# Attention weights of a graph layer: one exponential of the shifted score, or the larger of two exponentials with a bias per partition

## The chip, the core and the metric

The kernel runs on one core of a Trainium2 chip. The metric is device time in microseconds; 2156.93 us is the median of three runs of the kernel before (2154.71 to 2158.30).

## What is computed

A block of a graph network on 1250 nodes and 41250 edges: a layer norm, then two graph attention layers beside a linear-attention mixer, then a layer of 32 experts. The change is in the first attention layer alone, in what follows its projection h = x W (four heads of 512 columns). Of the reference this is:

```
e = jax.nn.leaky_relu(al_s[src] + al_d[dst], NEG_SLOPE)      # slope 0.2
m = jax.ops.segment_max(e, dst, num_segments=N)
ex = jnp.exp(e - m[dst])
denom = jax.ops.segment_sum(ex, dst, num_segments=N)
alpha = ex / (denom[dst] + 1e-16)
msg = h[src] * alpha[:, :, None]
out = jax.ops.segment_sum(msg, dst, num_segments=N)          # then + b1, then elu
```

The kernel does this densely. A matrix of edge counts c[s, d] is made earlier; the weight of source s for destination d is c[s, d] * exp(leaky(al_s[s] + al_d[d]) - m[d]), and the sum over sources is a matrix product. A column of ones beside h gives the denominator.

## The kernel before

The phases of the program follow each other; within one, each engine has its own instruction queue, and semaphores connect them. The phase of the change is gat1_phase. It makes 40 tiles: 4 heads of 10 tiles t, each with P = 125 destinations. A global number g = 10 hd + t counts them. For a tile:

- SyncE (SP) loads the counts cnt of the tile, 125 sources by 10 groups by 125 destinations (L1194 by way of L101 and L102), and, a head ahead, two rows broadcast to all partitions: al_d and m for all 1250 nodes (load_rows, L1180 and L1182). At the start it loads the whole bias brow (L1177); in the first head it also loads the weights of the second layer (L1358).
- VectorE, scores: u = al_s + al_d row (L1231), the leaky maximum max(0.2 u, u) (L1233), e = u - m row (L1235). Each is one pass over 125x1250. al_s differs by partition and group, the rows by destination.
- ScalarE: e = exp(e) in place, one instruction of 125x1250 (L1290).
- VectorE, weights: wt = e * cnt (L1243), a fourth pass of 125x1250.
- TensorE, aggregate: Z = sum over the ten groups of wt times h, in two halves of 256 and 257 columns (L1327), 20 products of float32 (40 records in the trace).
- VectorE, normalise: 1/denominator (L1250, L1251), o = Z * that + bias (L1252, L1254), mn = min(o, 0) (L1258). ScalarE: exp(mn) (L1303). VectorE, elu: o = max(exp(mn) - 1, o) (L1263).
- TensorE, turn: four transposes of o (L1337). ScalarE: copy of them out of PSUM to oT (L1307), then it issues the store to h1T_dram (L1309).

The order in each queue is written out by hand. In step t, VectorE does scores(t+2), normalise(t), weights(t+2), elu(t); ScalarE the exponential of tile t+2 (exp_scores), exp(mn) of tile t, the copy of tile t; TensorE aggregate(t+1), turn(t). The e, wt, cnt, o, mn, Z and oT buffers are double. The function heads runs this for head 0, then for heads 1 and 2 in a hardware loop (Fori) with one pass, then for head 3. Its waits count: exp_scores(t) waits for e_ready, weights(t) for exp_done, aggregate(t) for w_ready, and ScalarE's copy of tile t for turned, which the transposes of tile t raise.

Of the kernel before, what the change touches and what calls it, by code (L numbers as in the profile page):

```python
# [15 lines left out]
NT = 10  # L16
# [1123 lines left out]
def gat1_phase(nc, cx, b1, h, al, alT_dram, mT_dram, c_dram, h1T_dram, ident, W2, wa2, w2, w2_loaded, ext_ready):  # L1140


    (e_ready, exp_done, w_ready, agg, mn_ready, exp_mn, elu_ready, turned, t_evac, dve_step, b_loaded) = (
        cx.sem("gat1_" + s) for s in
        ("e_ready", "exp_done", "w_ready", "agg", "mn_ready", "exp_mn", "elu_ready", "turned", "t_evac", "dve_step",
# [6 lines left out]
    with ExitStack() as st:  # L1152
        brow = sb(nc, st, "gat1_brow", [128, F1])
        rows = [sb(nc, st, f"gat1_rows{b}", [128, 2, N]) for b in range(2)]
        u = sb(nc, st, "gat1_u", [P, NT, P])
# [11 lines left out]
        def heads(eng, body):  # L1167

            body(0, 0, True, False)
            with eng.Fori(0, H1 // 2 - 1) as i:  # L1170
                body(i * 2 + 1, 1, False, False)
                body(i * 2 + 2, 0, False, False)
            body(H1 - 1, 1, False, True)

        @block.sync
        def _(sp):
            sp.dma_start(brow[:], b1.partition_broadcast(128)).then_inc(b_loaded, 16)  # L1177

# [19 lines left out]
            heads(sp, body)  # L1198
# [7 lines left out]
        def _(dve):  # L1206
            def steps(before):

                made = [0]

                def step(ins):
                    made[0] += 1
                    ins.then_inc(dve_step, 1)
                    dve.wait_ge(dve_step, before + made[0])
                return step

            STEPS = 5
# [3 lines left out]
            dve.wait_ge(b_loaded, 16)


            def scores(hd, t, hb):
                b, g = t % 2, hd * NT + t
                step = steps(2 * g if isinstance(g, int) and g < 2 else g * STEPS - 6)
                if t == 0:
                    dve.wait_ge(rows_loaded[hb], (hd - hb) * 16 + 32)
                if not (isinstance(g, int) and g == 0):
                    dve.wait_ge(e_ready, g)  # L1230
# [51 lines left out]
            heads(dve, body)  # L1282

        @block.scalar
        def _(act):
            act.sem_inc(t_evac, 2)

            def exp_scores(hd, t):
                act.wait_ge(e_ready, hd * NT + (t + 1))
                act.activation(e[t % 2][:], e[t % 2][:], ACT.Exp).then_inc(exp_done, 1)  # L1290
# [21 lines left out]
            heads(act, body)  # L1312
# [4 lines left out]
        def _(pe):  # L1317
# [3 lines left out]
            def aggregate(hd, t):  # L1321
# [28 lines left out]
            heads(pe, body)  # L1350
# [1257 lines left out]
```

## Time and profile before

| what | value |
|---|---|
| median of three runs | 2156.93 us |
| the profiled execution, its own time | 2157.98 us |
| its span in the trace | 2156.3 us |
| TensorE busy over the span | 2021.0 us (94%) |
| VectorE | 1202.9 us (56%) |
| ScalarE | 448.0 us (21%) |
| the phase of the change, bias load to last copy | 861.9 to 1247.7 us |

The trace is of one execution, taken by the hardware profiler; all its times are counted from the start of the span. The span lies 1.7 us below the execution's own time. A row in order of time gives the start, the length, the engine, the line, the operation and its tiles, and in brackets the idle time of the engine before it with what ended it. A row that merges several instructions ends in a count. Shares of busy time are means over phases with different limits; for the phase of the change, a table by stretches gives the busy time of each engine there. A busy TensorE is one whose records follow without a gap, with its granted clock beside it.

### The profile page before, as it was taken

What the parts mean: (1) busy time and instruction counts of PE and PEld (TensorE: products, weight loads), DVE (VectorE), ACT (ScalarE), POOL (GpSimd) and SP (SyncE); (2) the same over time, 40 slices, a digit from 0 to 9 for tenths busy, and PEclk for the clock granted to TensorE, in tenths of its full rate; (3) what the DMA queues carried; (4) which work ended last, traced back from release to release, by engine and by line L of the source; (5) the groups of instructions that cost most, each with busy time, mean ns of one, the idle gap of its engine ahead of it and who ended that gap; (6) DMA issues with size and microseconds to landing.
All of it is one profiled execution on the core that took longest, in us unless ns stands there. A gap on an engine that the chain in (4) does not pass through costs nothing. (4 is left out here: it accounts for less than half of the span.)

```text
span 2156.3 us, 33575 instructions
## 1 busy us (share of the span) xinstructions
PE 2021.0 (94%) x10041; PEld 1479.3 (69%) x10042; DVE 1202.9 (56%) x2661; ACT 448.0 (21%) x822; POOL 183.1 (8%) x179
## 2 busy tenths in 40 slices
PE   4999899999999999799999979988996999999998
PEld 3666566666656888688888845545654777777776
DVE  5766436764375662788888742146765333333343
ACT  2212212122102321122222200003331222222222
POOL 0000000000000000000000000001001233233232
PEclk9999899999999999899999989998996999999999
DMA  7000130002436430743333244333405888898754
GB/s 254 16 16 19 64 123 19 16 16 85 150 111 194 146 117 1 246 152 99 122 97 95 70 159 166 133 112 105 146 29 201 251 244 248 239 293 274 203 128 86
DMA packets 81182, 282.66 MB, mean 131 GB/s; under 512 B 11690, under 2 KB 32226, under 8 KB 71491
## 3 DMA queue, kind: packets, MB, share of 16 engines
q1 hardware_dynamic: 59282, 211.66, 29.6%
q0 software_dynamic: 14848, 56.18, 10.7%
q10 hardware_dynamic: 6960, 13.62, 1.8%
q8 instruction: 55, 0.90, 0.2%
q14 instruction: 37, 0.30, 0.0%
HBM read 217.43 MB, written 63.99 MB: 131 GB/s over the span
## 5 line engine op out<-in xcount | busy, mean ns | idle before, releaser
L1327 PE MATMUL gat_Z<-h,gat_wt 125*125 125x256 f32 (+1 forms) x1600 | 354.9, 380 | 17.8 <-DVE gat_wt L1243 17.8
L1327 PEld LDWEIGHTS gat_Z<-h,gat_wt 125*125 125x125 f32 x1600 | 297.5, 188 | 63.7 <-DVE gat_wt L1243 18.2
L732 PE MATMUL mix_G<-mix_w,xnT 128*125 128x384 f32 x720 | 243.7, 489 | 0.0
L732 PEld LDWEIGHTS mix_G<-mix_w,xnT 128*125 128x125 f32 x720 | 133.6, 190 | 85.4 <-issue 3.1
L2091 PE MATMUL gat_Z<-h,gat_wt 125*125 125x384 f32 (+1 forms) x400 | 135.4, 496 | 13.0 <-DVE gat_wt L1830 13.0
L2331 DVE TENSOR_SCALAR ex_idS<-ex_ids 128x1 int32 x52 | 8.0, 154 | 215.1 <-DMA out_rows<-ex_y,ex_idS 215.1
L639 DVE SCALAR_TENSOR_TENSOR mix_count_A<-count_ikey,count_off,keyT 128x512 f32 x120 | 90.2, 751 | 56.4 <-issue 48.4
L2091 PEld LDWEIGHTS gat_Z<-h,gat_wt 125*125 125x125 f32 x400 | 75.0, 191 | 66.5 <-DVE gat_wt L1830 13.6
L2418 PE MATMUL ex_PH<-ex_xT,w_and_experts 128*128 128x128 f32 x936 | 113.0, 280 | 1.7 <-issue 0.7
L2418 PE MATMUL ex_PH<-ex_xT,ex_w 128*128 128x128 f32 x936 | 111.0, 277 | 1.1 <-issue 0.2
L645 DVE TENSOR_SCALAR mix_count_B<-count_islo,sloT 128x314 f16 x480 | 112.0, 298 | 0.0
L2418 PEld LDWEIGHTS ex_PH<-ex_xT,w_and_experts 128*128 128x128 f32 x936 | 108.4, 195 | 2.7 <-issue 2.6
L2428 PE MATMUL ex_PY<-ex_w,ex_hT 128*128 128x384 f32 x312 | 107.5, 494 | 1.3 <-ACT ex_hT L2365 1.3
L2428 PE MATMUL ex_PY<-w_and_experts,ex_hT 128*128 128x384 f32 x312 | 107.6, 495 | 1.0 <-ACT ex_hT L2365 0.7
L2418 PEld LDWEIGHTS ex_PH<-ex_xT,ex_w 128*128 128x128 f32 x936 | 106.5, 192 | 1.8 <-issue 1.8
L2301 DVE SCALAR_TENSOR_TENSOR ex_Q<-posm,offs,ex_iota 125x1280 bf16<-125x1280 f32 x54 | 83.8, 1552 | 38.8 <-issue 38.8
L2280 POOL DMA_INDIRECT out_rows<-ex_y,ex_idS x52 | 82.6, 1588 | 268.2 <-DVE ex_y L2333 223.3
L780 PE MATMUL mix_count_S<-mix_count_B,mix_count_A 128*128 x480 | 87.5, 300 | 5.1 <-DVE mix_count_B L645 2.8
L1557 PE MATMUL gat2p_X<-w_and_experts,gat2p_hT 128*125 128x386 f32 x240 | 81.2, 495 | 11.3 <-DMA gat2p_hT<-h1T_dram 11.3
L2373 ACT ACTIVATE ex_y<-ex_PY,ex_gate 128x384 f32<-128x384 f32 x52 | 30.2, 581 | 276.6 <-DMA out_rows<-ex_y,ex_idS 235.1
L2428 PEld LDWEIGHTS ex_PY<-ex_w,ex_hT 128*128 128x128 f32 x312 | 57.1, 190 | 39.6 <-ACT ex_hT L2365 2.2
L2428 PEld LDWEIGHTS ex_PY<-w_and_experts,ex_hT 128*128 128x128 f32 x312 | 57.1, 190 | 39.4 <-ACT ex_hT L2365 1.9
(346 smaller groups left out, 2974.2 us busy)
## 6 DMA issues: line engine op xcount, KB each, us to landing
w_and_experts<-in_L_ffn_W SPq DMA_DIRECT2D x32, 1152.0 KB, 8.1
ex_w<-in_L_ffn_W SPq DMA_DIRECT2D x32, 1152.0 KB, 7.9
gat_cnt<-c_dram SPq DMA_DIRECT2D x50, 546.9 KB
h1T_dram<-gat_oT ACTq DMA_DIRECT2D x40, 250.0 KB
gat2p_hT<-h1T_dram SPq DMA_DIRECT2D x10, 1000.0 KB, 6.5
mix_w<-in_L_mix_qkv_w SPq DMA_DIRECT2D x6, 1152.0 KB, 13.1
ct_dram<-mix_count_out SPq DMA_DIRECT2D x40, 157.0 KB, 2.0
mix_w_slice<-in_L_gnn_W SPq DMA_DIRECT2D x6, 1024.0 KB, 12.1
```

Of the source, the lines that this page charges most:

```text
L639: dve.scalar_tensor_tensor(CA[:, bass.ds(s * RB, RB), :], ikey[:].unsqueeze(1).to_broadcast([128, RB, 128]), off[:, win:win + 1], keyT[:, ...
L645: last = dve.tensor_scalar(CB[:, bass.ds(s * RB + b, 1), :], islo[:].unsqueeze(1), sloT[:, bass.ds(r * RB + b, 1)], None, ALU.is_equal)
L732: last = pe.matmul(G[c][:], xnT[:, k, t * P:(t + 1) * P], w[:, k, c, :], start=(k == 0), stop=(k == KD - 1))
L780: last = pe.matmul(S[:], CA[:, bass.ds(s * RB + b, 1), :].rearrange("p o k -> p (o k)"), CB[:, bass.ds(s * RB + b, 1), :].rearrange("p o k ...
L1327: last = pe.matmul(Z[b][j][:], wt[b][:, s, :], h[0:P, bass.ds(hd, 1), s, j * HC:(j + 1) * HC + j], start=(s == 0), stop=(s == NT - 1))
L1557: last = pe.matmul(bank[:, 0:W], stationary[:, k * P:(k + 1) * P], moving[:, k, :], start=fresh and k == 0, stop=k == KH - 1, skip_group_c ...
L2091: last = pe.matmul(Z[b][j][:], wt[b][:, s, :], h2[:, s, 386 * j:386 * j + CW[j]], start=(s == 0), stop=(s == NT - 1))
L2280: pool.indirect_dma_start(out, bass.IndirectOffsetOnAxis(ap=idS[:, 0:1], axis=0), y[:], None, compute_op=ALU.add).then_inc(added, 16)
L2301: dve.scalar_tensor_tensor(Q[:], posm[:, :, bass.ds(e, 1)].to_broadcast([P, NT, SLOT]), 1.0 if first else offs[:, bass.ds(at, 1)], iot[:]. ...
L2373: act.activation(y[:, 384:768], PY[1][:], ACT.Copy, scale=gate[:, slot]).then_inc(y_a, 1)
L2418: last = pe.matmul(PH[m][:], w1[b][:, k, m * 128:(m + 1) * 128], xT[:, k, :], start=(k == 0), stop=(k == KD - 1))
L2428: last = pe.matmul(PY[j][:], hT[:, k, :], w2[b][:, k, j * 384:(j + 1) * 384], start=(k == 0), stop=(k == KM - 1))
```

## The change

The weight is written another way. exp is increasing, so exp(max(u, 0.2 u) - m) is the larger of exp(u - m) and exp(0.2 u - m). With u = al_s + al_d these are exp(al_s + (al_d - m)) and exp(0.2 al_s + (0.2 al_d - m)): in each group of sources al_s is one number per partition, which an instruction of ScalarE can take as its bias.

- Once a head, shifted_rows makes the rows al_d - m and 0.2 al_d - m out of the loaded rows, in place, with two VectorE passes of 128x1250; for the next head this stands in step 5, ahead of normalise(5). Once a phase, al02 = 0.2 al_s is made (125x40).
- exp_scores makes e and f, ten instructions each of 125x125, one for each group, with al or al02 as bias.
- VectorE's scores are gone. weights first takes the larger of e and f, waits for it, and then multiplies by cnt.
- The bias is loaded a head at a time (128x512 in place of 128x2048), the next head's in step 5; VectorE waits for it in the first normalise of a head and no longer at the start. The rows of the head after next wait for the exponentials of a head (exp_done) in place of its scores (e_ready).
- The head loop is written out for all four heads, on all engines.

```diff
-        def heads(eng, body):
-
-            body(0, 0, True, False)
-            with eng.Fori(0, H1 // 2 - 1) as i:
-                body(i * 2 + 1, 1, False, False)
-                body(i * 2 + 2, 0, False, False)
-            body(H1 - 1, 1, False, True)
+        def heads(body):
+
+            for hd in range(H1):
+                body(hd, hd % 2, hd == 0, hd == H1 - 1)
...
-            sp.dma_start(brow[:], b1.partition_broadcast(128)).then_inc(b_loaded, 16)
+            def load_bias(hd):
+                sp.dma_start(brow[:, hd % 2, :], b1[hd * C1:(hd + 1) * C1].partition_broadcast(128)).then_inc(b_loaded, 16)
+
+            load_bias(0)
...
-                        sp.wait_ge(e_ready, hd * NT)
+                        sp.wait_ge(exp_done, hd * NT)
                     load_rows(hd + 1, 1 - b)
                 for t in range(NT):
+                    if t == NT // 2 and not last:
+                        if not first:
+                            sp.wait_ge(mn_ready, hd * NT + 2)
+                        load_bias(hd + 1)
...
-                step(dve.tensor_tensor(u[:], al[:, :, bass.ds(hd, 1)].to_broadcast([P, NT, P]),
-                                       rows[hb][0:P, 0:1, t * P:(t + 1) * P].to_broadcast([P, NT, P]), ALU.add))
-                step(dve.scalar_tensor_tensor(u[:], u[:], SLOPE, u[:], ALU.mult, ALU.max))
-                dve.wait_ge(w_ready, g + 1)
-                dve.tensor_tensor(e[b][:], u[:], rows[hb][0:P, 1:2, t * P:(t + 1) * P].to_broadcast([P, NT, P]),
-                                  ALU.subtract).then_inc(e_ready, 1)
+            step(dve.tensor_scalar(al02[:], al[:, :, 0:H1], SLOPE, None, ALU.mult))
+
+            def shifted_rows(hd, hb):
+                dve.wait_ge(rows_loaded[hb], (hd - hb) * 16 + 32)
+                step(dve.scalar_tensor_tensor(rows[hb][:, 1, :], rows[hb][:, 0, :], SLOPE, rows[hb][:, 1, :], ALU.mult,
+                                              ALU.subtract))
+                dve.scalar_tensor_tensor(rows[hb][:, 0, :], rows[hb][:, 0, :], 1.0 - SLOPE, rows[hb][:, 1, :], ALU.mult,
+                                         ALU.add).then_inc(r_ready, 1)
 
             def weights(hd, t):
                 b, g = t % 2, hd * NT + t
                 dve.wait_ge(exp_done, g + 1)
                 dve.wait_ge(c_loaded[b], hd * (2 * HT16) + 32 * (t // 2 + 1))
+                step(dve.tensor_tensor(e[b][:], e[b][:], f[b][:], ALU.max))
                 dve.wait_ge(agg, g + 1)
                 dve.tensor_tensor(wt[b][:], e[b][:], cnt[b][:], ALU.mult).then_inc(w_ready, 1)
...
                 for t in range(NT):
-                    if t + 2 < NT:
-                        scores(hd, t + 2, hb)
-                    elif not last:
-                        scores(hd + 1, t + 2 - NT, 1 - hb)
-                    normalise(hd, t, max(0, t + 3 - NT) if last else 0)
+                    if t == NT // 2 and not last:
+                        shifted_rows(hd + 1, 1 - hb)
+                    normalise(hd, t)
...
             def exp_scores(hd, t):
-                act.wait_ge(e_ready, hd * NT + (t + 1))
-                act.activation(e[t % 2][:], e[t % 2][:], ACT.Exp).then_inc(exp_done, 1)
+                g, b = hd * NT + t, t % 2
+                act.wait_ge(r_ready, hd + 1)
+                act.wait_ge(w_ready, g + 1)
+                for s in range(NT):
+                    act.activation(e[b][:, s, :], rows[hd % 2][0:P, 0, t * P:(t + 1) * P], ACT.Exp, bias=al[:, s, hd:hd + 1])
+                    last = act.activation(f[b][:, s, :], rows[hd % 2][0:P, 1, t * P:(t + 1) * P], ACT.Exp,
+                                          bias=al02[:, s, hd:hd + 1])
+                last.then_inc(exp_done, 1)
```

How the queues stand, first ScalarE in its steady steps. Before: the exponential of the tile two ahead, exp(mn), the copy of the turned tile, its store, and the next step's exponential.

```order
L1290 ACTIVATE gat_e<-gat_e 125x1250
L1303 ACTIVATE gat_mn<-gat_mn 125x512
L1307 ACTIVATE gat_oT<-gat_T 128x500
L1309 DMA h1T_dram<-gat_oT 128x500
L1290 ACTIVATE gat_e<-gat_e 125x1250
```

ScalarE after, from the last two of a tile's twenty exponentials to the first two of the next tile's (al02 shows as gat_al).

```order
L1279 ACTIVATE gat_e<-gat_rows,al 125x125
L1280 ACTIVATE gat_f<-gat_rows,gat_al 125x125
L1295 ACTIVATE gat_mn<-gat_mn 125x512
L1299 ACTIVATE gat_oT<-gat_T 128x500
L1301 DMA h1T_dram<-gat_oT 128x500
L1279 ACTIVATE gat_e<-gat_rows,al 125x125
L1280 ACTIVATE gat_f<-gat_rows,gat_al 125x125
```

Between one store and the next exp(mn), one instruction has become twenty; exp(mn), copy and store keep their places.

VectorE in a steady step, before: three passes of scores, five instructions of normalise, weights, elu.

```order
L1231 TENSOR_TENSOR gat_u<-al,gat_rows 125x1250
L1233 SCALAR_TENSOR_TENSOR gat_u<-gat_u 125x1250
L1235 TENSOR_TENSOR gat_e<-gat_u,gat_rows 125x1250
L1250 TENSOR_SCALAR gat_rden<-gat_Z 125x1
L1251 RECIPROCAL gat_rden<-gat_rden 125x1
L1252 SCALAR_TENSOR_TENSOR gat_o<-gat_Z,gat_rden,gat_brow 125x256
L1254 SCALAR_TENSOR_TENSOR gat_o<-gat_Z,gat_rden,gat_brow 125x256
L1258 TENSOR_SCALAR gat_mn<-gat_o 125x512
L1243 TENSOR_TENSOR gat_wt<-gat_e,gat_cnt 125x1250
L1263 SCALAR_TENSOR_TENSOR gat_o<-gat_mn,gat_o 125x512
```

The same step after.

```order
L1238 TENSOR_SCALAR gat_rden<-gat_Z 125x1
L1239 RECIPROCAL gat_rden<-gat_rden 125x1
L1240 SCALAR_TENSOR_TENSOR gat_o<-gat_Z,gat_rden,gat_brow 125x256
L1242 SCALAR_TENSOR_TENSOR gat_o<-gat_Z,gat_rden,gat_brow 125x256
L1246 TENSOR_SCALAR gat_mn<-gat_o 125x512
L1228 TENSOR_TENSOR gat_e<-gat_e,gat_f 125x1250
L1230 TENSOR_TENSOR gat_wt<-gat_e,gat_cnt 125x1250
L1251 SCALAR_TENSOR_TENSOR gat_o<-gat_mn,gat_o 125x512
```

The three passes ahead of normalise are gone, and a pass (the maximum of e and f) stands between normalise and the multiply, ahead of elu.

## Rows read from the trace of the kernel before

**Rows 1.** Stretches: us; busy PE, PEld, DVE, ACT, POOL; granted clock; DMA share, GB/s.
```profile
960.00:1040.00 80.00, 80.00 (x389) 69.19 (x388) 69.72 (x90) 21.16 (x27) 0.00 (x0) 1.00 0.34 103
```

**Rows 2.** One tile in time: start, us, engine, line, operation [idle before <-releaser].
```profile
1080.03 8.82 PE L1327 MATMUL gat_Z<-h,gat_wt 125*125 125x256 f32 x40
...
1080.22 0.59 ACT L1307 ACTIVATE gat_oT<-gat_T 128x500 f32<-128x500 f32 x1 [6.33 <-PE gat_T L1337]
...
1081.21 1.25 ACT L1290 ACTIVATE gat_e<-gat_e 125x1250 f32<-125x1250 f32 x1 [0.40 <-ACT gat_oT L1307]
1082.37 0.61 ACT L1303 ACTIVATE gat_mn<-gat_mn 125x512 f32<-125x512 f32 x1
1082.49 1.46 DVE L1243 TENSOR_TENSOR gat_wt<-gat_e,gat_cnt 125x1250 f32<-125x1250 f32 x1 [0.97 <-ACT gat_e L1290]
1083.87 0.69 DVE L1263 SCALAR_TENSOR_TENSOR gat_o<-gat_mn,gat_o 125x512 f32<-125x512 f32 x1
...
1088.68 0.59 PE L1337 MATMUL gat_T<-ident,gat_o 125*128 125x125 f32 x4
...
1089.31 0.59 ACT L1307 ACTIVATE gat_oT<-gat_T 128x500 f32<-128x500 f32 x1 [6.33 <-PE gat_T L1337]
```

**Rows 3.** The same view: copy of tile 0, and the last tiles.
```profile
898.53 0.59 ACT L1307 ACTIVATE gat_oT<-gat_T 128x500 f32<-128x500 f32 x1 [6.41 <-PE gat_T L1337]
...
1234.64 0.59 ACT L1307 ACTIVATE gat_oT<-gat_T 128x500 f32<-128x500 f32 x1 [6.33 <-PE gat_T L1337]
...
1245.72 0.69 DVE L1263 SCALAR_TENSOR_TENSOR gat_o<-gat_mn,gat_o 125x512 f32<-125x512 f32 x1 [0.70 <-ACT gat_mn L1303]
...
1246.47 0.65 PE L1337 MATMUL gat_T<-ident,gat_o 125*128 125x125 f32 x4 [2.78 <-DVE gat_o L1263]
1247.15 0.59 ACT L1307 ACTIVATE gat_oT<-gat_T 128x500 f32<-128x500 f32 x1 [1.46 <-PE gat_T L1337]
```

**Rows 4.** The same view: the start of the stage.
```profile
861.92 0.36 SPq L1177 DMA_DIRECT2D gat_brow<-in_L_gnn_b  x1
...
870.83 1.46 DVE L1231 TENSOR_TENSOR gat_u<-al,gat_rows 125x1250 f32<-125x1250 f32 x1 [9.83 <-DMA gat_rows<-mT_dram]
872.33 1.46 DVE L1233 SCALAR_TENSOR_TENSOR gat_u<-gat_u 125x1250 f32<-125x1250 f32 x1
...
878.37 19.69 PE L1327 MATMUL gat_Z<-h,gat_wt 125*125 125x256 f32 x80 [17.83 <-DVE gat_wt L1243]
...
889.73 0.15 DVE L1250 TENSOR_SCALAR gat_rden<-gat_Z 125x1 f32<-125x1 f32 x1
```

**Rows 5.** ScalarE by shape: line, shapes, count | busy us, mean ns | idle before.
```profile
L2365 ACT ACTIVATE ex_hT<-ex_PH,ex_b1T 128x128 f32<-128x128 f32 x156 | 54.0, 366 | 101.9 <-PE ex_PH L2418 91.8 <-issue 10.1
L1290 ACT ACTIVATE gat_e<-gat_e 125x1250 f32<-125x1250 f32 x40 | 49.9, 1246 | 44.2 <-DVE gat_e L1235 29.0 <-ACT gat_oT L1307 15.2
...
L1303 ACT ACTIVATE gat_mn<-gat_mn 125x512 f32<-125x512 f32 x40 | 24.6, 614 | 1.9 <-DVE gat_mn L1258 1.9
...
L308 ACT ACTIVATE xn<-xa,shift,rstd 125x768 f32<-125x768 f32 x10 | 10.0, 1021 | 7.3 <-DVE shift L240 7.3
...
L2055 ACT ACTIVATE rt_gate<-rt_gate 125x128 f32<-125x128 f32 x1 | 0.3, 292 | 0.0
```

**Rows 6.** In order of time, ScalarE alone: three neighbours merged into one row.
```profile
20.53 2.87 ACT L308 ACTIVATE xn<-xa,shift,rstd 125x768 f32<-125x768 f32 x3 [7.26 <-DVE shift L240]
```

**Rows 7.** Table by stretches around two idle gaps of TensorE, columns as rows 1.
```profile
556.00:557.70 1.70, 0.01 (x1) 0.01 (x1) 1.01 (x3) 0.00 (x0) 0.00 (x0) 1.00 0.00 0
557.70:559.00 1.30, 1.27 (x10) 1.30 (x11) 0.41 (x1) 0.41 (x1) 0.00 (x0) 0.78 0.19 26
559.00:562.50 3.50, 3.50 (x10) 2.29 (x9) 0.69 (x2) 0.56 (x2) 0.00 (x0) 0.59 1.03 227
...
1755.80:1757.10 1.30, 0.02 (x1) 0.00 (x0) 1.01 (x5) 0.82 (x3) 0.00 (x0) 1.00 1.01 428
1757.10:1760.00 2.90, 2.90 (x13) 2.05 (x14) 1.93 (x5) 0.95 (x3) 2.44 (x2) 1.00 1.05 367
```

More of the change, by code:

```diff
@@ L1140, in gat1_phase @@
 def gat1_phase(nc, cx, b1, h, al, alT_dram, mT_dram, c_dram, h1T_dram, ident, W2, wa2, w2, w2_loaded, ext_ready):
[L1143 removed]
+    (r_ready, exp_done, w_ready, agg, mn_ready, exp_mn, elu_ready, turned, t_evac, dve_step, b_loaded) = (
         cx.sem("gat1_" + s) for s in
[L1145 removed]
+        ("r_ready", "exp_done", "w_ready", "agg", "mn_ready", "exp_mn", "elu_ready", "turned", "t_evac", "dve_step",
          "b_loaded"))
@@ L1152, in gat1_phase @@
     with ExitStack() as st:
-        brow = sb(nc, st, "gat1_brow", [128, F1])
+        brow = sb(nc, st, "gat1_brow", [128, 2, C1])
         rows = [sb(nc, st, f"gat1_rows{b}", [128, 2, N]) for b in range(2)]
-        u = sb(nc, st, "gat1_u", [P, NT, P])
+        al02 = sb(nc, st, "gat1_al02", [P, NT, H1])
+        f = [sb(nc, st, f"gat1_f{b}", [P, NT, P]) for b in range(2)]
         e = [sb(nc, st, f"gat1_e{b}", [P, NT, P]) for b in range(2)]
@@ L1206, in _ @@
         def _(dve):
[L1207 to L1217, printed above, removed]
+            step = Chain(dve, dve_step)
             for freed in (w_ready, mn_ready):
                 dve.sem_inc(freed, 2)
[L1221 to L1230, printed above, removed]
-                step(dve.tensor_tensor(u[:], al[:, :, bass.ds(hd, 1)].to_broadcast([P, NT, P]),
-                                       rows[hb][0:P, 0:1, t * P:(t + 1) * P].to_broadcast([P, NT, P]), ALU.add))
-                step(dve.scalar_tensor_tensor(u[:], u[:], SLOPE, u[:], ALU.mult, ALU.max))
-                dve.wait_ge(w_ready, g + 1)
-                dve.tensor_tensor(e[b][:], u[:], rows[hb][0:P, 1:2, t * P:(t + 1) * P].to_broadcast([P, NT, P]),
-                                  ALU.subtract).then_inc(e_ready, 1)
+            step(dve.tensor_scalar(al02[:], al[:, :, 0:H1], SLOPE, None, ALU.mult))
[5 more added lines that the diff above has]
+                                         ALU.add).then_inc(r_ready, 1)
             def weights(hd, t):
@@ L1241, in weights, with normalise @@
                 dve.wait_ge(c_loaded[b], hd * (2 * HT16) + 32 * (t // 2 + 1))
+                step(dve.tensor_tensor(e[b][:], e[b][:], f[b][:], ALU.max))
                 dve.wait_ge(agg, g + 1)
                 dve.tensor_tensor(wt[b][:], e[b][:], cnt[b][:], ALU.mult).then_inc(w_ready, 1)
-            def normalise(hd, t, left):
+            def normalise(hd, t):
                 b, g = t % 2, hd * NT + t
-                step = steps(g * STEPS + (6, 4, 2)[left])
+                if t == 0:
+                    dve.wait_ge(b_loaded, 16 * (hd + 1))
                 dve.wait_ge(agg, g + 3)
@@ L1252, in normalise @@
                 dve.scalar_tensor_tensor(o[b][:, 0:HC], Z[b][0][:], rden[b][:],
-                                         brow[0:P, bass.ds(hd * C1, HC)], ALU.mult, ALU.add)
+                                         brow[0:P, hd % 2, 0:HC], ALU.mult, ALU.add)
                 step(dve.scalar_tensor_tensor(o[b][:, HC:C1], Z[b][1][:, 0:HC], rden[b][:],
-                                              brow[0:P, bass.ds(hd * C1 + HC, HC)], ALU.mult, ALU.add))
+                                              brow[0:P, hd % 2, HC:C1], ALU.mult, ALU.add))
                 if not (isinstance(g, int) and g == 0):
@@ L1263, in elu @@
                 dve.scalar_tensor_tensor(o[b][:], mn[b][:], -1.0, o[b][:], ALU.add, ALU.max).then_inc(elu_ready, 1)
+            shifted_rows(0, 0)
             for t in range(2):
-                scores(0, t, 0)
                 weights(0, t)
```

10 lines of the change are left out of this document (5 added, 5 removed).

## The prediction

> **What bounds the kernel now.** I read the views in this order: a table by stretches for the stage of the change, one steady tile of it in order of time, its first and last tiles, then the rows that price ScalarE instructions.
>
> The table [rows 1] shows 80 us from the middle of the first aggregation: TensorE is busy for all 80.00 us at a granted clock of 1.00 (2.4 GHz), VectorE for 69.72, ScalarE for 21.16. So VectorE is loaded to 87% but does not set the pace, and passes taken from it are not time taken from the kernel, unless something downstream of VectorE is late.
>
> One tile in order of time [rows 2] shows why nothing is late. The copy of the turned tile (L1307) starts at 1080.22 and the next one at 1089.31: a period of 9.09 us. From [rows 3], (1234.64 - 898.53) / 37 = 9.08 us over 37 tiles. Inside it TensorE runs one product of 8.82 us and four transposes; VectorE and ScalarE work beside it, and ScalarE waits 6.33 us for the transposes.
>
> The same rows hold a second loop, which now has slack. ScalarE's queue takes, for tile t: exponential of tile t+2, exponential of mn(t), copy of the turned tile t. The copy waits for turn(t), so **the exponential of tile t+3 stands behind the copy of tile t, that is behind turn(t)**. VectorE's queue takes normalise(t+1), weights(t+3), elu(t+1); so elu(t+1) stands behind the weights, which wait for that exponential. And turn(t+1) on TensorE waits for elu(t+1). This closes: turn(t), copy, exponential, weights, elu, turn(t+1). Before the change, counted from the start of the copy [rows 2]: exponential starts at 0.99, elu at 1083.87 - 1080.22 = 3.65 and ends at 4.34. The product of TensorE ends only at 1088.85. The next transposes start at 8.46, so about 4.1 us of slack lie in the loop, and that is all that the change can add to it free of charge.
>
> **The change part by part.**
>
> *VectorE loses two passes a tile and keeps two.* Before: add, leaky maximum, subtract, multiply, each about 1.46 us. After: a maximum and a multiply, both two-tensor passes of 125x1250, for which the multiply's 1.46 us [rows 2] is the price. About 2.9 us a tile go. The passes that go lay between elu and the next normalise, outside the loop above, beside a busy TensorE; their removal is worth 0 in steady state. The maximum that comes is inside the loop, with a wait for its end before the multiply: 1.50 us from start to start, as the two dependent passes at 870.83 and 872.33 show [rows 4].
>
> *ScalarE gains.* One exponential of 125x1250 becomes twenty of 125x125, each with a bias read per partition. No row has that form on SBUF data, so I bound it. Below: the exponential of 125x128 without a bias operand took 292 ns [rows 5], and neighbours overlap: the three instructions at 20.53 take 2.87 us while one takes 1.02 [rows 6, 5], so start to start is (2.87 - 1.02) / 2 = 0.925 us and the overlap about 0.095. That gives 0.20 us start to start and 0.29 for one. Above: the same 125x768 instructions carry two per-partition operands; from 1250 and 512 elements [rows 5] one element costs (1246 - 614) / 738 = 0.856 ns, so 643 elements fewer leave 0.925 - 0.550 = 0.375 us start to start, 0.47 for one. One operand lies in the middle: 768 elements without operands would be 614 + 256 x 0.856 = 833 ns, two operands made it 1021, so one is worth 94 ns, and 125 elements with one come to 292 - 3 + 94 = 383 ns, near the 366 ns that the one-operand 128x128 instruction on PSUM data took [rows 5]. I take 0.383 for one and 0.290 start to start. Twenty: 19 x 0.290 + 0.383 = **5.89 us** in place of 1.25; by the bounds 4.09 and 7.60.
>
> The Trainium skill ("ScalarE: Activation LUTs", section "What ACT_TABLE_LOAD costs") states 280 ns + 0.833 ns an element for an instruction with a bias pointer and an overlap of about 93 ns, by which the twenty would take 5.92 us and the period below would be 11.2 us as well. The skill also has a rule that speaks against the change: "VectorE: DVE Perf Modes", section on the TRN2 errata, says that an operation on SBUF data pays a fixed time per instruction, so that one large tile pays once and many small tiles pay each time, and advises tiles of 512 elements or more. Rows 5 agree: 1250 elements in one instruction cost 1246 ns, ten times 128 elements would cost 2920.
>
> *The loop after.* Copy to first exponential 0.99 (as now, with the store's issue between), twenty exponentials 5.89, release 0.03 (1081.21 + 1.25 to 1082.49 [rows 2]), maximum 1.50, multiply to elu 1.38 (1082.49 to 1083.87), elu 0.69 [rows 3], release 0.06 and transposes to the next copy 0.68 (1246.41 to 1246.47 to 1247.15 [rows 3], where the transposes waited for elu as they would here). Sum 0.99 + 5.89 + 0.03 + 1.50 + 1.38 + 0.69 + 0.06 + 0.68 = **11.22 us**. That exceeds the 9.08 of TensorE, so the loop becomes the bound: 2.14 us a tile. The product still starts right behind the transposes, since its weights were made a period earlier, and then TensorE idles some 1.8 us until elu. mn's exponential, now behind the twenty, ends at 0.99 + 5.89 + 0.6 = 7.5, ahead of elu at 9.8: hidden by the two passes. The loop runs from the copy of tile 0 to the copy of tile 37 (the exponentials of tiles 3 to 39): 37 x 2.14 = **79.2 us**. By the bounds 9.42 and 12.93 us a period: 12.6 and 142.5.
>
> *The start.* VectorE began at 870.83 when the rows landed, TensorE at 878.37 [rows 4]: 7.54 us. After: two passes that shift the rows 2 x 1.49, twenty exponentials 5.89, release 0.03, maximum and multiply 2.99 make 11.9 us: +4.4. The bias load ahead of the rows shrinks, by its shape, from 1024 to 256 KB; 1024 + 1250 KB took the 8.91 us from 861.92 to 870.83, so 768 KB less are worth up to 768 / 2274 x 8.9 = 3.0 us, nothing if the other loads fill the gap. I take **+2.5**, between 1.4 and 4.4. The second tile's weights come 8.8 us after the first's, hidden by the first product (878.37 to 889.73, 11.36 us after an idle 17.83 [rows 4]).
>
> *Costed at nothing.* The row shift for the next head (two passes, three times) sits before normalise(5): it moves that from the head of a period by 3 us, while the weights behind it wait until 6.9 anyway; if the twenty took 2 us, that cover would be gone and it would cost 1 us, three times. On SP, the row loads of a head now wait for the last exponential of the head before instead of its scores, and cnt loads are queued behind; the cnt of that tile has one period, 11.2 us, to land, and in the start's rows 2274 KB took 8.9 us against 1250 + 625 KB here. The bias loads stand mid-head, before one cnt load, with their condition long true. The head loop written out four times: tiles cross the loop's ends at the same 9.08 us now [rows 3], so no branch time is there to win.
>
> *The sum.* 79.2 + 2.5 = 81.7 us on the profiled execution's own 2157.98 (its span is 2156.3; the median of the runs shown, 2156.93, is 1 us less): 2239.7, and against the median 2238.6. I predict **2239**.
>
> **The rivals.**
>
> *Exponentials nearly as cheap as without an operand* (the lower bound): period 9.42, 12.6 us and about 0.7 at the start: 2171. For it: the operand's price rests on a two-operand row. Against: 366 ns on the only one-operand row of this size.
>
> *No loss at all.* The place is the same loop; the point from which it decides is twenty exponentials in 5.89 - 2.14 = 3.75 us, 0.18 us each: then TensorE's 9.08 stays the bound, the start is even (11.9 - 2.1 - 3.0 against 7.54), and the time is 2157. Slack left over buys nothing, since TensorE was full already [rows 1]. Against it: the lower bound is 0.20.
>
> *No overlap*, or an operand at twice the price (the upper bound): period 12.93, 142.5 + 4: 2304. Against: the overlap is seen with operands [rows 6].
>
> *TensorE's clock falls in the new gaps.* After an idle 1.70 us the granted clock was 0.78 and then 0.59 for 3.5 us, means of its levels 2.4 and 1.2 GHz; after an idle 1.30 us it stayed 1.00 [rows 7]. The new gap of 1.8 is like the first. But a product at 0.59 for 3.5 us and 0.78 for 1.3 loses 1.7 us, about the gap itself, so it still ends before elu; only transposes of 0.65 at 0.78 lie on the path: 0.2 x 37 = 7 us. With every product as slow as the first (11.36), a period is 11.36 + 0.26 = 11.6 and the time 2254. It widens the range upward and decides nothing.
>
> **How the numbers follow.** Forecast with its clock variants 0.83; cheap exponentials 0.07; no loss 0.03; no overlap 0.07. The range goes from 2215 (0.26 us start to start, one at 0.355, an even start: period 10.63, +57) to 2262 (0.31 us, period 11.60, 4.4 at the start and the clock's 7: +104); what it leaves out of the rivals is 0.17. A measurement of this kernel can tell about 0.2% from no change, 4.3 us: faster 0.01, same 0.02, slower 0.97.
>
> **What would show it.** In the changed kernel's profile, copies of the turned tile 11.2 us apart; twenty exponentials in 5.9 us starting 1.0 us after each copy; VectorE's maximum waiting for them; TensorE idle some 1.8 us a tile before its transposes, released by elu; VectorE busy only near half of the stage. If exponentials start every 0.20 us or less, or the idle time of TensorE is not put down to elu, the forecast is wrong.

## The result and the profile after

The changed kernel takes 2241.57 us (median of four runs, 2238.03 to 2244.00), the kernel before 2156.55 beside it; the ratio is 1.0393, with a 95% interval of 1.0375 to 1.0411. It is slower by 85 us; 2239 was forecast. The profiled execution took 2238.03 us, its span is 2236.3, so the trace has 80.0 us more than that of before to account for. One of the ten runs of the reordered kernel below took 2703 us at a granted clock of 0.735 in place of 0.97; its ratio and interval are of the other nine.

One steady tile of the changed kernel in order of time (start, length, engine, line, operation, idle before it with its releaser), against [rows 2]:

```profile
1091.06 8.82 PE L1319 MATMUL gat_Z<-h,gat_wt 125*125 125x256 f32 x40
...
1091.26 0.59 ACT L1299 ACTIVATE gat_oT<-gat_T 128x500 f32<-128x500 f32 x1 [3.81 <-PE gat_T L1329]
...
1092.31 0.40 ACT L1279 ACTIVATE gat_e<-gat_rows,al 125x125 f32<-125x125 f32 x1 [0.46 <-ACT gat_oT L1299]
...
1097.83 0.38 ACT L1280 ACTIVATE gat_f<-gat_rows,gat_al 125x125 f32<-125x125 f32 x1
1098.12 0.61 ACT L1295 ACTIVATE gat_mn<-gat_mn 125x512 f32<-125x512 f32 x1
1098.24 1.46 DVE L1228 TENSOR_TENSOR gat_e<-gat_e,gat_f 125x1250 f32<-125x1250 f32 x1 [6.08 <-ACT gat_f L1280]
1099.74 1.46 DVE L1230 TENSOR_TENSOR gat_wt<-gat_e,gat_cnt 125x1250 f32<-125x1250 f32 x1
1101.12 0.68 DVE L1251 SCALAR_TENSOR_TENSOR gat_o<-gat_mn,gat_o 125x512 f32<-125x512 f32 x1
...
1101.86 0.65 PE L1329 MATMUL gat_T<-ident,gat_o 125*128 125x125 f32 x4 [1.97 <-DVE gat_o L1251]
...
1102.54 0.59 ACT L1299 ACTIVATE gat_oT<-gat_T 128x500 f32<-128x500 f32 x1 [3.81 <-PE gat_T L1329]
```

The copy of the turned tile (now L1299) stands at 1091.26 and 1102.54: a period of 11.28 us in place of 9.09. The chain between is the one foretold. The first exponential starts 1.05 us after the copy, the twentieth ends at 1098.21, the maximum starts 0.03 later, then multiply, elu and transposes, each released by the one before. The product of TensorE, 8.82 us as before, has ended at 1099.88, and TensorE idles 1.97 us until elu lets the transposes go. Copy to first exponential 1.05, exponentials 5.90, release 0.03, maximum 1.50, multiply 1.38, elu and release 0.74, transposes to copy 0.68: 11.28.

The table by stretches of the same kernel (columns as in [rows 1]):

```profile
960.00:1040.00 80.00, 69.55 (x314) 57.72 (x313) 35.41 (x56) 50.13 (x159) 0.00 (x0) 0.96 0.32 97
```

TensorE is busy for 69.55 us of 80 where it was busy for all of them [rows 1], at a mean granted clock of 0.96; VectorE has fallen from 69.72 to 35.41, ScalarE has risen from 21.16 to 50.13. No engine is full, as it is when a chain of waits sets the pace. Who waited for whom in the phase (us in total, times, longest):

```profile
DVE gat_e L1228 <- ACT gat_f L1280: 225.6, 39, 6.5
...
PE gat_T L1329 <- DVE gat_o L1251: 56.4, 38, 2.8
```

VectorE's maximum waited 225.6 us for the exponentials, and TensorE's transposes 56.4 us for elu. Before, VectorE waited for its exponential too, but for 0.97 us a tile [rows 2], and in the steady tiles the transposes followed the product without a gap [rows 1].

The start, the copy of tile 0, that of tile 37 and the last one, against [rows 3, 4]:

```profile
858.88 0.36 SPq L1176 DMA_DIRECT2D gat_brow<-in_L_gnn_b  x1
...
867.44 1.46 DVE L1219 SCALAR_TENSOR_TENSOR gat_rows<-gat_rows 128x1250 f32<-128x1250 f32 x1 [8.14 <-DMA gat_rows<-mT_dram]
...
870.43 0.40 ACT L1279 ACTIVATE gat_e<-gat_rows,al 125x125 f32<-125x125 f32 x1 [15.12 <-DVE gat_rows L1221]
...
876.36 1.46 DVE L1228 TENSOR_TENSOR gat_e<-gat_e,gat_f 125x1250 f32<-125x1250 f32 x1 [5.97 <-ACT gat_f L1280]
...
879.37 19.02 PE L1319 MATMUL gat_Z<-h,gat_wt 125*125 125x256 f32 x80 [21.90 <-DVE gat_wt L1230]
...
898.85 0.59 ACT L1299 ACTIVATE gat_oT<-gat_T 128x500 f32<-128x500 f32 x1 [6.63 <-PE gat_T L1329]
...
1316.91 0.59 ACT L1299 ACTIVATE gat_oT<-gat_T 128x500 f32<-128x500 f32 x1 [3.81 <-PE gat_T L1329]
...
1329.41 0.59 ACT L1299 ACTIVATE gat_oT<-gat_T 128x500 f32<-128x500 f32 x1 [1.46 <-PE gat_T L1329]
```

From the copy of tile 0 to that of tile 37 there are 418.06 us, 11.30 a tile, where before there were 336.11: **+81.95**. From the first load of the phase to the copy of tile 0 there are 39.97 us in place of 36.61: **+3.36**. The rest is outside: the phase began 3.04 us earlier in this execution, and what follows the last copy took 2.2 us less. In the runs below the phase begins anywhere from 855.4 to 861.7 with the same code ahead of it, and what follows the last copy takes 907.6 to 912.9 us in those whose expert phase does the same work, so neither is put down to the change. 81.95 + 3.36 - 3.04 - 2.2 is the 80.0, to the rounding.

### The profile page after: what moved, and what is told of

Read it like the earlier page. It is cut to its first block and busy times, and to the rows that moved or that the text cites. A ratio compares the mean times of both kernels' runs of the same rounds, so it can differ in the third digit from the quotient of the medians.

```text
span 2236.3 us, 34292 instructions
## 1 busy us (share of the span) xinstructions
PE 2045.3 (91%) x10041; PEld 1489.2 (67%) x10042; DVE 1101.5 (49%) x2590; ACT 634.8 (28%) x1582; POOL 182.2 (8%) x179
## 5 line engine op out<-in xcount | busy, mean ns | idle before, releaser
L1319 PE MATMUL gat_Z<-h,gat_wt 125*125 125x256 f32 (+1 forms) x1600 | 374.0, 395 | 21.9 <-DVE gat_wt L1230 21.9
L1319 PEld LDWEIGHTS gat_Z<-h,gat_wt 125*125 125x125 f32 x1600 | 311.0, 196 | 73.6 <-DVE gat_wt L1230 22.3
L1228 DVE TENSOR_TENSOR gat_e<-gat_e,gat_f 125x1250 f32<-125x1250 f32 x40 | 58.4, 1461 | 225.6 <-ACT gat_f L1280 225.6
L1279 ACT ACTIVATE gat_e<-gat_rows,al 125x125 f32<-125x125 f32 x400 | 154.3, 386 | 32.5 <-ACT gat_oT L1299 17.3
L1280 ACT ACTIVATE gat_f<-gat_rows,gat_al 125x125 f32<-125x125 f32 x400 | 153.7, 384 | 0.0
L2083 PEld LDWEIGHTS gat_Z<-h,gat_wt 125*125 125x125 f32 x400 | 75.0, 191 | 66.6 <-DVE gat_wt L1822 13.7
L639 DVE SCALAR_TENSOR_TENSOR mix_count_A<-count_ikey,count_off,keyT 128x512 f32 x120 | 90.2, 751 | 56.4 <-issue 48.5
```

Of the source, the lines that this page charges most:

```text
L639: dve.scalar_tensor_tensor(CA[:, bass.ds(s * RB, RB), :], ikey[:].unsqueeze(1).to_broadcast([128, RB, 128]), off[:, win:win + 1], keyT[:, ...
L1279: act.activation(e[b][:, s, :], rows[hd % 2][0:P, 0, t * P:(t + 1) * P], ACT.Exp, bias=al[:, s, hd:hd + 1])
L1280: last = act.activation(f[b][:, s, :], rows[hd % 2][0:P, 1, t * P:(t + 1) * P], ACT.Exp, bias=al02[:, s, hd:hd + 1])
L1319: last = pe.matmul(Z[b][j][:], wt[b][:, s, :], h[0:P, hd, s, j * HC:(j + 1) * HC + j], start=(s == 0), stop=(s == NT - 1))
L2083: last = pe.matmul(Z[b][j][:], wt[b][:, s, :], h2[:, s, 386 * j:386 * j + CW[j]], start=(s == 0), stop=(s == NT - 1))
```

## The experiments

The theory: the changed kernel's pace is that of the loop copy, twenty exponentials, maximum, multiply, elu, transposes, copy. The rivals: the longer written-out program costs time; the work of ScalarE as such does; TensorE itself is slower, by its clock.

### The head loop alone

```diff
-            body(0, 0, True, False)
-            with eng.Fori(0, H1 // 2 - 1) as i:
...
+            for hd in range(H1):
+                body(hd, hd % 2, hd == 0, hd == H1 - 1)
```

> The kernel before with nothing changed but the head loop, written out for four heads. The theory (the loop copy, twenty exponentials, maximum, multiply, elu, transposes sets the pace of the changed kernel): the loop's form has no part in the loss, so the time is that of before, 2157 us, within 4, and the copies of the turned tile stand 9.08 us apart. The rival (some of the 85 us comes from the longer instruction stream): 2160 us or more, with idle time of TensorE put down to no engine.

Measured: 2155.44 us against 2157.45 for the kernel before beside it, ratio 0.9992 (0.9979 to 1.0006). The copies of tiles 0 and 37 in order of time:

```profile
896.22 0.59 ACT L1304 ACTIVATE gat_oT<-gat_T 128x500 f32<-128x500 f32 x1 [6.10 <-PE gat_T L1334]
...
1232.33 0.59 ACT L1304 ACTIVATE gat_oT<-gat_T 128x500 f32<-128x500 f32 x1 [6.33 <-PE gat_T L1334]
```

336.11 us for 37 tiles, to the hundredth that of before. The written-out loop costs nothing and saves nothing that these runs can tell.

### The same work in another order

```diff
                     normalise(hd, t)
+                    elu(hd, t)
                     if t + 2 < NT:
                         weights(hd, t + 2)
                     elif not last:
                         weights(hd + 1, t + 2 - NT)
-                    elu(hd, t)
...
             exp_scores(0, 1)
+            exp_scores(0, 2)
...
-                    if t + 2 < NT:
-                        exp_scores(hd, t + 2)
-                    elif not last:
-                        exp_scores(hd + 1, t + 2 - NT)
...
                     act.activation(mn[b][:], mn[b][:], ACT.Exp).then_inc(exp_mn, 1)
+                    if t + 3 < NT:
+                        exp_scores(hd, t + 3)
+                    elif not last:
+                        exp_scores(hd + 1, t + 3 - NT)
```

> The changed kernel with the same instructions in another order: on ScalarE the exponential of mn(t) first, then the twenty exponentials of tile t+3 (one tile further ahead) and then the copy of the turned tile t; on VectorE elu(t) ahead of weights(t+2). The theory: the twenty exponentials and the two passes leave the loop, TensorE is the bound again at 9.08 us a tile, and only the later start (about 4 us) stays: 2161 us, between 2156 and 2166. The rival (ScalarE's or VectorE's work as such, or its traffic, costs the time): ScalarE's 7.7 us of work a tile is the same, so the time stays near 2240.

Measured: 2158.24 us against 2157.45, ratio 1.0003 (0.9989 to 1.0017). The copies of the turned tile are 9.08 us apart (899.43 to 1235.54, 336.11 us for 37 tiles), and the loss is gone; the later start, 40.13 us from the first load to the copy of tile 0 against 36.61, is left and lies inside the interval. The table by stretches of this kernel:

```profile
960.00:1040.00 80.00, 80.00 (x389) 69.19 (x388) 47.94 (x74) 61.34 (x193) 0.00 (x0) 1.00 0.35 107
```

TensorE is full again at a clock of 1.00, with ScalarE at 61.34 us of 80, more than the changed kernel shows for the same stretch since it now makes a tile every 9.08 us. A tile in order of time:

```profile
1081.13 0.59 ACT L1300 ACTIVATE gat_oT<-gat_T 128x500 f32<-128x500 f32 x1 [1.26 <-PE gat_T L1330]
...
1082.46 0.63 ACT L1292 ACTIVATE gat_mn<-gat_mn 125x512 f32<-125x512 f32 x1 [0.75 <-DVE gat_mn L1246]
1083.00 0.39 ACT L1279 ACTIVATE gat_e<-gat_rows,al 125x125 f32<-125x125 f32 x1
1083.13 0.69 DVE L1251 SCALAR_TENSOR_TENSOR gat_o<-gat_mn,gat_o 125x512 f32<-125x512 f32 x1 [0.70 <-ACT gat_mn L1292]
...
1083.73 1.46 DVE L1228 TENSOR_TENSOR gat_e<-gat_e,gat_f 125x1250 f32<-125x1250 f32 x1
...
1085.22 1.46 DVE L1230 TENSOR_TENSOR gat_wt<-gat_e,gat_cnt 125x1250 f32<-125x1250 f32 x1
...
1088.50 0.39 ACT L1280 ACTIVATE gat_f<-gat_rows,gat_al 125x125 f32<-125x125 f32 x1
...
1089.58 0.59 PE L1330 MATMUL gat_T<-ident,gat_o 125*128 125x125 f32 x4
...
1090.21 0.59 ACT L1300 ACTIVATE gat_oT<-gat_T 128x500 f32<-128x500 f32 x1 [1.32 <-PE gat_T L1330]
```

exp(mn) comes first (1082.46), elu right behind it (1083.13), the maximum does not wait since the exponentials of its tile were made a step earlier, and the twenty that run from 1083.00 to 1088.89 are for the tile after. They end before the transposes at 1089.58 that release the next copy. The same twenty instructions, in the same number, cost 82 us in one order and nothing in the other. So neither ScalarE's work nor its traffic is the cause; the place in the queue is. The bias loaded a head at a time, the later wait of the row loads and the row shift are all in this kernel as well, so they cost no time a tile either. Three moves were made together here; the next experiment takes VectorE's apart from ScalarE's two, which were not tried one by one.

### One of the moves alone

```diff
                     normalise(hd, t)
+                    elu(hd, t)
                     if t + 2 < NT:
                         weights(hd, t + 2)
                     elif not last:
                         weights(hd + 1, t + 2 - NT)
-                    elu(hd, t)
```

> The changed kernel with one move alone: on VectorE elu(t) ahead of weights(t+2); ScalarE's order as it is. The theory: elu no longer waits for the two passes, but its exponential still stands behind the twenty, and the weights now come after elu. The pace is then set by a loop over two tiles: copy, exponentials, elu, maximum, multiply, product, transposes. 1.05 + 5.90 + 0.62 + 0.70 + 1.50 + 1.50 + 8.82 + 0.65 is 20.7 us for two tiles, 10.4 us for one: 1.3 above 9.08, so 48 us and 4 at the start, 2209 us, between 2198 and 2222. The rival (elu's place is what the loop hangs on alone): 2161.

Measured: 2206.73 us against 2157.45, ratio 1.0223 (1.0191 to 1.0255). Two tiles in order of time:

```profile
1066.97 0.59 ACT L1299 ACTIVATE gat_oT<-gat_T 128x500 f32<-128x500 f32 x1 [5.79 <-PE gat_T L1329]
...
1073.83 0.61 ACT L1295 ACTIVATE gat_mn<-gat_mn 125x512 f32<-125x512 f32 x1
...
1074.47 0.69 DVE L1251 SCALAR_TENSOR_TENSOR gat_o<-gat_mn,gat_o 125x512 f32<-125x512 f32 x1 [6.20 <-ACT gat_mn L1295]
...
1075.08 1.46 DVE L1228 TENSOR_TENSOR gat_e<-gat_e,gat_f 125x1250 f32<-125x1250 f32 x1
...
1076.06 0.59 ACT L1299 ACTIVATE gat_oT<-gat_T 128x500 f32<-128x500 f32 x1 [1.62 <-PE gat_T L1329]
1076.57 1.46 DVE L1230 TENSOR_TENSOR gat_wt<-gat_e,gat_cnt 125x1250 f32<-125x1250 f32 x1
...
1078.09 8.92 PE L1319 MATMUL gat_Z<-h,gat_wt 125*125 125x256 f32 x40 [2.07 <-DVE gat_wt L1230]
...
1087.47 0.59 ACT L1299 ACTIVATE gat_oT<-gat_T 128x500 f32<-128x500 f32 x1 [3.95 <-PE gat_T L1329]
```

From copy to copy two tiles on, 1066.97 to 1087.47, there are 20.50 us: the forecast 20.7, alternately 9.09 and 11.41 a tile. elu runs at 1074.47, but only when exp(mn) has come out from behind the twenty (it waited 6.20 us for it), and now the product at 1078.09 waits 2.07 us for the weights. Taking elu out from behind the two passes gives back 0.98 us of the 2.2 a tile (381.7 us for 37 tiles, 10.32 a tile); the rest hangs on the exponentials' place in ScalarE's queue.

### Four exponentials fewer

```diff
+            for b in range(2):
+                step(dve.memset(f[b][:, 6:NT, :], 0.0))
...
                 for s in range(NT):
-                    act.activation(e[b][:, s, :], rows[hd % 2][0:P, 0, t * P:(t + 1) * P], ACT.Exp, bias=al[:, s, hd:hd + 1])
-                    last = act.activation(f[b][:, s, :], rows[hd % 2][0:P, 1, t * P:(t + 1) * P], ACT.Exp,
-                                          bias=al02[:, s, hd:hd + 1])
+                    last = act.activation(e[b][:, s, :], rows[hd % 2][0:P, 0, t * P:(t + 1) * P], ACT.Exp, bias=al[:, s, hd:hd + 1])
+                    if s < 6:
+                        act.activation(f[b][:, s, :], rows[hd % 2][0:P, 1, t * P:(t + 1) * P], ACT.Exp,
+                                       bias=al02[:, s, hd:hd + 1])
```

> The changed kernel with four of a tile's twenty exponentials left out (f is made for six of the ten groups of sources, and is zero in the rest, so the weights there are those of the positive branch alone). The theory: each exponential left out takes 0.29 us from the period until 9.08 is reached. 11.30 - 1.16 = 10.14 us, 43 us less over 37 tiles: 2198 us, between 2190 and 2206. The rival (the time goes to TensorE's clock, or to waits that do not hang on the exponentials): under half of that, above 2220.

Measured: 2205.22 us against 2157.45, ratio 1.0216 (1.0193 to 1.0238). The copies of tiles 0 and 37:

```profile
901.03 0.59 ACT L1302 ACTIVATE gat_oT<-gat_T 128x500 f32<-128x500 f32 x1 [6.63 <-PE gat_T L1332]
...
1275.57 0.59 ACT L1302 ACTIVATE gat_oT<-gat_T 128x500 f32<-128x500 f32 x1 [3.81 <-PE gat_T L1332]
```

374.54 / 37 = 10.12 us, the forecast 10.14: the period follows the number of exponentials at 0.29 us each. The total is 7 us above the expectation's middle, and that lies behind the phase: from the last copy to the end there are 916.2 us where the changed kernel had 906.9. The expert phase made 53 turns (rounds of its loop) in place of 52, as its activations show, three a turn (x159 here, x156 in [rows 5]), and a turn takes some 9.5 us there. That the experts got other nodes because the weights differ is the likely reason and was not looked into:

```profile
L2360 ACT ACTIVATE ex_hT<-ex_PH,ex_b1T 128x128 f32<-128x128 f32 x159 | 54.4, 367 | 100.0 <-PE ex_PH L2413 89.8 <-issue 9.9
```

### No bias operand

```diff
-                    act.activation(e[b][:, s, :], rows[hd % 2][0:P, 0, t * P:(t + 1) * P], ACT.Exp, bias=al[:, s, hd:hd + 1])
-                    last = act.activation(f[b][:, s, :], rows[hd % 2][0:P, 1, t * P:(t + 1) * P], ACT.Exp,
-                                          bias=al02[:, s, hd:hd + 1])
+                    act.activation(e[b][:, s, :], rows[hd % 2][0:P, 0, t * P:(t + 1) * P], ACT.Exp)
+                    last = act.activation(f[b][:, s, :], rows[hd % 2][0:P, 1, t * P:(t + 1) * P], ACT.Exp)
```

> The changed kernel with the twenty exponentials made without their per-partition bias (the source's part of the score is left out of the weights). It measures the disputed price: by the prediction's rows one operand costs 94 ns, and without it an exponential of 125x125 would take 0.29 us and start 0.20 us after its neighbour. Then the twenty take 4.1 us, the period is 9.48 us and the time 67 us less: 2174 us, between 2165 and 2182. The rival (the instruction's fixed part is the same with and without the operand): 2240, no change.

Measured: 2182.64 us against 2155.07, ratio 1.0123 (1.0103 to 1.0144). The exponentials by shape (count, busy us, mean ns), first of this kernel, then of the changed one:

```profile
L1279 ACT ACTIVATE gat_e<-gat_rows 125x125 f32<-125x125 f32 x400 | 117.2, 293 | 31.7 <-ACT gat_oT L1298 17.3 <-DVE gat_rows L1221 14.4
L1280 ACT ACTIVATE gat_f<-gat_rows 125x125 f32<-125x125 f32 x400 | 116.6, 291 | 0.0
```

```profile
L1279 ACT ACTIVATE gat_e<-gat_rows,al 125x125 f32<-125x125 f32 x400 | 154.3, 386 | 32.5 <-ACT gat_oT L1299 17.3 <-DVE gat_rows L1221 15.1
L1280 ACT ACTIVATE gat_f<-gat_rows,gat_al 125x125 f32<-125x125 f32 x400 | 153.7, 384 | 0.0
```

The operand costs 385 - 292 = 93 ns, the price that the prediction worked out from two-operand rows as 94. The Trainium skill ("ScalarE: Activation LUTs", section "What ACT_TABLE_LOAD costs") states about 93 ns for a pointer operand, and 280 ns + 0.833 ns an element with one, an estimate of 384 for 125 elements: the trace agrees, with 93 and 385. The copies of tiles 0 and 37:

```profile
899.94 0.59 ACT L1298 ACTIVATE gat_oT<-gat_T 128x500 f32<-128x500 f32 x1 [6.63 <-PE gat_T L1328]
...
1248.98 0.59 ACT L1298 ACTIVATE gat_oT<-gat_T 128x500 f32<-128x500 f32 x1 [3.81 <-PE gat_T L1328]
```

349.04 / 37 = 9.43 us, within 0.05 of the expectation and at the prediction's lower bound, 9.42. The total lies 8.6 us above the expectation's middle and 0.6 us outside its range, again by what is behind the phase: from the last copy to the end there are 921.7 us, with 53 turns here too. One turn more explains some 9.5 us of the 14.8 above the changed kernel; the rest was not followed up.

### The gaps filled

```diff
+        spare = pb(nc, st, "gat1_spare", [P, HC])
...
             def turn(hd, t):
                 b, g = t % 2, hd * NT + t
+                if 1 <= g <= H1 * NT - 3:
+                    for s in range(3):
+                        pe.matmul(spare[:], ident[0:P, 0:P], h[0:P, hd, s, 0:HC], start=True, stop=True)
                 pe.wait_ge(elu_ready, g + 1)
```

> The changed kernel with three more products of 256 columns a tile on TensorE, into a bank that nobody reads, ahead of the transposes, where TensorE waits for elu. They add 1.3 us of work to 9.08, still under the period. The theory (the loop past TensorE sets the pace, and a fall of the clock in the gaps is nearly hidden): the time stays, 2240 within 6, or falls by up to 7 us if the clock stays at 2.4 GHz and the transposes on the path run faster for it. The rival (TensorE's own time, at a lower clock, is what is paid): 37 x 1.3 us more, 2288.

Measured: 2241.66 us, ratio 1.0403 (1.0383 to 1.0424) to the kernel before; the changed kernel has 1.0393. The table by stretches, and one gap in TensorE's order of time:

```profile
960.00:1040.00 80.00, 75.25 (x356) 63.20 (x356) 36.42 (x58) 49.06 (x154) 0.00 (x0) 1.00 0.32 97
```

```profile
1084.80 1.46 PE L1329 MATMUL gat_spare<-h,ident 125*125 125x256 f32 x6
1086.94 0.65 PE L1333 MATMUL gat_T<-ident,gat_o 125*128 125x125 f32 x4 [0.68 <-DVE gat_o L1252]
```

The three products take 1.46 us, the wait for elu shrinks to 0.68, and the granted clock is 1.00 throughout. The period stays: from 895.55 to 1313.17 there are 11.29 us a tile, 11.30 in the changed kernel. So TensorE has time to spare in the changed kernel, and its clock is not what was paid.

### The start of the kernel before

```diff
-            sp.dma_start(brow[:], b1.partition_broadcast(128)).then_inc(b_loaded, 16)
...
             load_rows(0, 0)
...
-                if not last:
-                    if not first:
-                        sp.wait_ge(e_ready, hd * NT)
+                if not last and not first:
+                    sp.wait_ge(e_ready, hd * NT)
                     load_rows(hd + 1, 1 - b)
...
                     rows_dma(sp, cnt[t % 2], c_dram[t, :, :].rearrange("p (t d) -> p t d", d=P), c_loaded[t % 2])
+                    if first and t == 1:
+                        sp.dma_start(brow[:], b1.partition_broadcast(128)).then_inc(b_loaded, 16)
+                        load_rows(1, 1)
...
-            dve.wait_ge(b_loaded, 16)
...
+                if isinstance(g, int) and g == 0:
+                    dve.wait_ge(b_loaded, 16)
```

> The kernel before with its start alone rearranged: the rows of head 0 and the counts of tiles 0 and 1 are loaded ahead of the whole bias and of the rows of head 1, and VectorE waits for the bias in the first normalise. The prediction gave up to 3.0 us for the bias load ahead of the rows; the changed kernel, with a bias a quarter as long, showed 8.56 us from the first load's issue to VectorE's first pass on the rows in place of 8.91. If the time to land goes by the bytes ahead, VectorE begins 3 to 4 us earlier and the time is 2153.5 us. If it goes by a delay that every load has, and not by the bytes ahead: under 1 us, 2156.

Measured: 2154.36 us against 2155.07, ratio 0.9996 (0.9985 to 1.0007): not to be told from no change. The start in order of time:

```profile
855.64 0.35 SPq L1179 DMA_DIRECT2D gat_rows<-alT_dram  x1
...
862.30 1.46 DVE L1230 TENSOR_TENSOR gat_u<-al,gat_rows 125x1250 f32<-125x1250 f32 x1 [7.58 <-DMA gat_rows<-mT_dram]
...
869.58 19.36 PE L1328 MATMUL gat_Z<-h,gat_wt 125*125 125x256 f32 x80 [15.32 <-DVE gat_wt L1242]
```

In the trace the gain is there: VectorE begins 6.66 us after the first load's issue in place of 8.91 [rows 4], and TensorE 13.94 in place of 16.45, 2.5 us earlier. That is 0.12% of the time, inside the interval. Neither of the two expectations was quite met; with the whole bias out of the way 2.25 us come back, not 3 to 4.

## Why the prediction was right

*The bound and the loop.* Right. TensorE was full, VectorE's passes were beside it, and taking them away was worth nothing: the reordered kernel has VectorE busy for 48 us of 80 in place of 70, and takes the time of before. The loop through elu was named with its order and its sum, 11.22 us; it measured 11.28. The 0.06 is the step from copy to first exponential, 1.05 in place of the 0.99 that stood before an exponential without an operand.

*The price of an exponential.* Right: 0.383 us and 0.290 from start to start were taken, 0.385 and 0.290 measured (5.90 us for the twenty, 5.89 forecast). The bounds 0.20 and 0.375 were wide, but the lower one is what the kernel without operands showed, 9.43 us a period for 9.42. The choice inside them, one operand at half the price of two, was what carried the number; no row of before showed it, and the kernel without operands did. The rule that the prediction weighed against the change, from "VectorE: DVE Perf Modes" in the Trainium skill, section on the TRN2 errata, held: 1250 elements cost 1246 ns in one instruction [rows 5], and the same 1250 cost 10 x 290 in ten. The 2920 that the prediction put beside it leaves out its own overlap: without operands, ten would have cost some 2100, at the 0.20 from start to start that the kernel without operands shows.

*The 37 tiles.* 79.2 forecast, 81.95 measured. Of the 2.75 us, 37 x 0.06 is 2.2. The first of the 37 periods took 11.68 us and two others 11.55 and 11.38; the rest lie at 11.27 to 11.31. Two of the three are the clock: the transposes on the path took 1.00 us in the first and 0.74 in the period of 11.38, where 0.65 is usual, and in the kernel with filled gaps these two periods took 11.33 and 11.28.

```profile
909.50 1.00 PE L1329 MATMUL gat_T<-ident,gat_o 125*128 125x125 f32 x4 [2.02 <-DVE gat_o L1251]
```

The period of 11.55 is as long in the filled kernel; its first exponential starts 1.32 us after the copy in place of 1.05, and why was not tried. The row shift, exp(mn) and the loads that were costed at nothing cost no more than its 0.28 us. (A tile's counts are 610 KB where the prediction's text has 625; nothing hangs on it.)

*The start.* Its size was off. Taken were +2.5 us, measured +4.04 to the first product (20.49 against 16.45 us from the first load) and +3.36 to the copy of tile 0. The step that failed is the shorter bias load, priced by its bytes at up to 3.0 and taken at 1.9: VectorE began 8.56 us after the first load's issue in place of 8.91, a gain of 0.35 (7.89 to 8.41 in five other kernels with the same loads, a gain of 0.5 to 1.0). The chain behind it was right: 867.44 to 879.37 is 11.93 us, 11.9 forecast. That the copy of tile 0 came only 3.36 later was not forecast: the first product took 10.36 us in this trace and 11.04 in that of before, at mean granted clocks of 0.86 and 0.80, and 10.66 to 11.84 in the five others.

*The rivals.* Cheap exponentials and no overlap fell with the 0.290. No loss fell with them. The clock did fall: twelve of 38 steady products in the trace of the changed kernel took over 10 us in place of 8.82. This one, in order of time, with the transposes behind it, and a stretch from within it (columns as in [rows 1]; a granted clock of 0.50, the 1.2 GHz level) show why it is nearly free:

```profile
1079.79 10.51 PE L1319 MATMUL gat_Z<-h,gat_wt 125*125 125x256 f32 x40
...
1090.58 0.65 PE L1329 MATMUL gat_T<-ident,gat_o 125*128 125x125 f32 x4 [0.29 <-DVE gat_o L1251]
```

```profile
1080.40:1083.60 3.20, 3.20 (x9) 2.46 (x9) 0.46 (x2) 2.74 (x10) 0.00 (x0) 0.50 0.22 80
```

The product ends at 1090.30, and the transposes still wait 0.29 us for elu: the slower product eats the gap and no more. The prediction allowed up to 7 us for transposes at the lower clock; the kernel with filled gaps, at 1.00, gained 0.01 us a tile, 0.4 in all, which is the two periods with slow transposes.

*The sum.* 2157.98 + 81.95 + 3.36 would be 2243.3 with nothing else different; the profiled execution lay 5.3 us below that by the phases around. The medians differ by 85.0 us and the phase by 81.95 + 3.36 = 85.3, so those 5.3 us are scatter of the profiled execution. The two misses, 2.75 and 0.9, go the same way and stay inside the range.

## What to carry to other kernels

When an engine beside the bound is relieved, nothing is won; when its work is moved to another queue, the question is what stands behind it there. Write down the cycle of waits through the queues, add up its durations, and compare with the period of the bound: the slack between is all that a longer step may use. If it does not fit, change the queue order before changing the work: here the exponential of mn ahead of the twenty, the twenty one tile further ahead, and elu ahead of the weights took all 82 us back with the same instructions.

## What the runs showed of the hardware beyond what was expected

- A shorter load ahead in the queue did not bring the next one forward in proportion to its bytes. With 1024 KB of bias ahead of the rows, the first pass on them began 8.91 us after the first issue, and 8.71 in the kernel with the loop written out; with 256 KB, 7.89 to 8.56 in the changed kernel and five others with the same loads; with none, 6.66, where other loads follow the rows as well. So the first 256 KB cost 1.2 to 1.9 us and the other 768 KB 0.2 to 1.0. Why was not tried.
- Idle gaps of much the same length were followed by a lower clock or not. In the changed kernel, with gaps of about 2 us a tile, twelve of 38 products ran long; mostly one after every second or third gap of 1.97 us; in the kernel with elu moved alone, products behind gaps of 2.06 or 2.07 us took 8.92 us (the one at 1078.09 at a granted clock of 1.00), and only those behind its two longest, 2.11 and 2.22, took 10.6; with four exponentials fewer, without operands and in the filled kernel the gaps are shorter, and every steady product took 8.82. What decides was not tried.
